# A graph network's attention pass: the second gather of each edge adds into the first by DMA, instead of a VectorE addition

## What is computed

```
x = x + _L2_gnn_ref(h, edge_attr_16, edge_attr_4, ..., edge_index)   # h: normalised x
# inside:
msg_s = (s_n @ Ws_src)[src] + (s_n @ Ws_dst)[dst]
msg_v = einsum(v_n, Wv_src)[src] + einsum(v_n, Wv_dst)[dst]
w1 = rbf @ W_rbf
m1_s, m1_v = _cg_tp(msg_s, msg_v, y0, y1, w1 ...)
a = leaky(m1_s @ W_alpha) * alpha_dot, summed by head      # scores
# values: two more linear maps, a gate and a second _cg_tp; softmax over the edges of a node; sum
```

## Time and profile before

| | |
|---|---|
| median of 3 runs | 6777.98 us |
| profiled execution, its own time | 6772.18 us |
| its span | 6767.9 us |
| PE busy | 6291.2 us (93%) |
| DVE busy | 4284.2 us (63%) |
| POOL busy | 4163.2 us (62%) |
| ACT busy | 2376.2 us (35%) |

### The profile page before, as it was taken

The page is one execution under the profiler, slowest core; times in us unless marked ns, Lnnn a source line. Parts: engine busy times, 40 slices in busy tenths (PEclk is TensorE's granted clock), DMA queues, the critical chain, the costliest instruction groups (busy, mean ns, idle before and its releaser), DMA issues. The chain is left out here.

```text
span 6767.9 us, 184764 instructions
## 1 busy us (share of the span) xinstructions
PE 6291.2 (93%) x57917; PEld 5076.0 (75%) x57917; DVE 4284.2 (63%) x11616; ACT 2376.2 (35%) x6454; POOL 4163.2 (62%) x4226
## 2 busy tenths in 40 slices
PE   6999999989999997999999999999288799999999
PEld 3788888777877775888888888888277448888887
DVE  5455555534444446999999999999488753333333
ACT  2122222212212124777777777777200121111111
POOL 1677777567777766777777777777000116666665
PEclk9999999989999997999999999999699559999999
DMA  1344444344444443333333333333167014444443
GB/s 60 111 120 124 124 123 122 108 114 129 127 123 129 126 106 87 97 96 95 95 97 96 95 95 97 96 95 96 52 185 194 4 47 115 115 115 115 115 116 97
DMA packets 735106, 719.47 MB, mean 106 GB/s; under 512 B 248938, under 2 KB 594266, under 8 KB 734338
## 3 DMA queue, kind: packets, MB, share of 16 engines
q1 hardware_dynamic: 546818, 396.43, 20.6%
q0 software_dynamic: 188160, 321.38, 19.0%
HBM read 557.59 MB, written 159.75 MB: 106 GB/s over the span
## 5 line engine op out<-in xcount | busy, mean ns | idle before, releaser
L892 POOL DMA_INDIRECT l_edge_g<-node_table,l_edge_idx x2352 | 2279.7, 969 | 1292.8 <-issue 944.1
L939 PEld LDWEIGHTS l_edge_win_ps<-l_edge_hot,l_edge_prod 128*128 128x128 f32 (+2 forms) x14112 | 1309.8, 149 | 218.2 <-issue 177.1
L939 PE MATMUL l_edge_win_ps<-l_edge_hot,l_edge_prod 128*128 128x40 f32 (+2 forms) x14112 | 1438.4, 255 | 36.0 <-DVE sums_T L752 24.7
L957 ACT ACTIVATE l_edge_h<-l_edge_h_ps 128x256 f32<-128x256 f32 (+1 forms) x784 | 342.9, 437 | 2753.0 <-PE l_edge_h_ps L913 2541.4
L1853 POOL DMA_INDIRECT att_g_dst<-node_table,att_ends x784 | 878.9, 1121 | 239.0 <-issue 239.0
L993 DVE TENSOR_TENSOR l_edge_prod<-l_edge_w_ps,l_edge_g 128x512 f32<-128x512 f32 x588 | 405.8, 690 | 961.3 <-PE l_edge_w_ps L920 812.2
L1851 POOL DMA_INDIRECT att_g<-node_table,att_ends x784 | 810.7, 1034 | 267.3 <-issue 238.1
L752 DVE TENSOR_TENSOR sums_T<-sums_T,l_edge_win_ps 128x160 f32 x588 | 189.4, 322 | 875.3 <-PE l_edge_win_ps L943 680.7
L1873 PE MATMUL att_turn<-ident,sums_T 128*128 128x128 f32 (+1 forms) x4704 | 690.0, 282 | 36.8 <-ACT sums_T L1958 29.9
L920 PEld LDWEIGHTS l_edge_w_ps<-l_edge_wo,l_edge_h 64*128 64x128 f32 (+1 forms) x4704 | 502.3, 190 | 286.9 <-issue 284.4
L1958 ACT ACTIVATE sums_T<-att_turn 128x512 f32<-128x512 f32 (+1 forms) x1176 | 661.8, 593 | 110.6 <-PE att_turn L1873 104.7
(11 more groups left out here) (272 smaller groups left out, 10086.0 us busy)
## 6 DMA issues: line engine op xcount, KB each, us to landing
l_edge_hot<-hot_tiles SPq DMA_DIRECT2D x392, 320.0 KB
hot_tiles<-l_edge_hot SPq DMA_DIRECT2D x196, 320.0 KB, 2.3
l_messages<-att_rows SPq DMA_DIRECT2D x196, 320.0 KB
sum_msg<-l_messages SPq DMA_DIRECT2D x196, 320.0 KB, 3.5
l_edge_g<-node_table,l_edge_idx POOLq DMA_INDIRECT x2352
att_ea<-in_edge_attr_T SPq DMA_DIRECT2D x196, 64.0 KB
att_g<-node_table,att_ends POOLq DMA_INDIRECT x784
att_g_dst<-node_table,att_ends POOLq DMA_INDIRECT x784
```

The costliest lines, as they stand in the source:

```text
L892: pool.indirect_dma_start(g[s][:, t, :], None, rows_of, bass.IndirectOffsetOnAxis(idx[s][:, t:t + 1], 0)).then_inc(fetched[s], 16)
L939: nc.tensor.matmul(at, q[:, t, lo:lo + width], to[:, t, kinds, :], start=t == 0, stop=t == TG - 1)
```

## The change

`g_dst` and DVE's `join` go. POOL first gathers all four source tiles of group i into `g[s]`. Then it waits until the source rows of group i-1 have landed, and issues four indirect DMAs that gather the destination rows of group i-1 and add them to `g` in flight (`compute_op=ALU.add`). The semaphore `joined` becomes four, one for each buffer, and counts landings of those DMAs (16 each); ACT, DVE and SP wait for it where they waited for `join` or for the fetch. POOL has one step more at the end.

```
-                g_dst = pair("g_dst", [P, TG, FEAT], n=FETCH)
-                joined = sem(ctx, "att_joined")
+                joined = [sem(ctx, f"att_joined{s}") for s in range(FETCH)]
...
-                                at_least(sp, fetched[s], 32 * TG * r)
+                                at_least(sp, joined[s], 16 * TG * r)
...
                                 for t in range(TG):
                                     pool.indirect_dma_start(g[s][:, t, :], None, table[2],
                                                             bass.IndirectOffsetOnAxis(ends[s][:, t:t + 1], 0)).then_inc(fetched[s], 16)
-                                    pool.indirect_dma_start(g_dst[s][:, t, :], None, table[3],
-                                                            bass.IndirectOffsetOnAxis(ends[s][:, TG + t:TG + t + 1], 0)
-                                                            ).then_inc(fetched[s], 16)
-
-                        steps(pool, NG, 0, step, warm=8, unroll=U)
+                            if live(i - 1, NG):
+                                s1, r1 = back(s, r, 1, U)
+                                gate(pool, (w_loaded, 16 * N_LOAD),
+                                     (fetched[s1], 16 * TG * (r1 + 1)))
+                                for t in range(TG):
+                                    pool.indirect_dma_start(g[s1][:, t, :], None, table[3],
+                                                            bass.IndirectOffsetOnAxis(ends[s1][:, TG + t:TG + t + 1], 0),
+                                                            compute_op=ALU.add).then_inc(joined[s1], 16)
+
+                        steps(pool, NG, 1, step, warm=8, unroll=U)
...
-                                 (joined, i + 1))
+                                 (joined[s], 16 * TG * (r + 1)))
...
-                        def join(i, s, r):
-                            at_least(dve, fetched[s], 32 * TG * (r + 1))
-                            tt(g[s][:, :, :], g[s][:, :, :], g_dst[s][:, :, :], ALU.add, joined)
-
...
-                            dve.wait_ge(joined, i + 1)
+                            at_least(dve, joined[s], 16 * TG * (r + 1))
...
-                        join(0, 0, 0)
-
...
-                            if live(i, NG) and live(i + 1, NG):
-                                join(i + 1, (s + 1) % U, r + (s + 1) // U)
...
-                        steps(dve, NG - 1, 4, step, warm=8, unroll=U)
+                        steps(dve, NG, 3, step, warm=8, unroll=U)
```

## The result

The changed kernel takes 7132.68 us (median of 4 runs, 7118.78 to 7139.69) against 6775.08 before (median of 4): a ratio of 1.0524, 95% interval 1.0505 to 1.0543, or 358 us more by the medians (355 by the ratio, which takes in all nine runs of the changed kernel). The forecast of 6782 was wrong, and so was the range, which ended at 7090. It is the first rival, POOL as the bound, that came true, above its likeliest value of 7003.

What follows compares the result with a forecast made beforehand. PE was taken to bound the kernel at 11.08 us a group. Profiled 6772.18 plus 4.2 for the start, other terms 0, gave 6776.4, or 6782 us against the median; range 6760 to 7090.

Steps and rivals of the forecast that it cites:

- the first rival: POOL's stream: adding DMAs lift its step above PE's 11.08 us a group; +225 us, 7003 us; chance 42%.
- PE paces before: Settled attention pass: PE sets the pace at 11.08 us a group, busy 10.85 and idle 0.23.
- The join is worth 0 on the path: DVE: removing 196 joins of 0.82 us only lengthens its wait for ACT's gate before `att_vec`; 0 us.
- The start, +4.2: Start of the pass: four more DMAs before group 0 (+5.0 us), less one join of 0.82; +4.2 us.
- The added wait and the later destination rows, 0: POOL's wait for source rows passes at once; destination rows land at 22.9 us, needed at 25.9; 0 us.
- The adding DMA, e of 0 to 0.19: POOL's extra time e per adding DMA over a plain one's 0.95 us, taken as 0 to 0.19 us.
- The break-even: POOL's step reaches PE's 11.08 us at e = 0.19, an adding DMA of 1.14 us.
- POOL's 10.31 without the extra: POOL's own time for eight plain DMAs a group, read between joins at the start of the pass: 10.31 us.
- The slower rival, 1.42 for three accesses instead of two: POOL's time goes by accesses described: adding DMA 1.42 us, e = 0.47, step 12.19; 7003 us; chance 42%.
- upper bound of e = 0.70: POOL's largest extra per adding DMA, from the longest gather of 1.647 us: +406 us, 7184 us.
- The transfer: DMA engines: ample room expected; a rival with adding DMAs ten times 0.32 us gave +575, 7357 us; chance 4%.
- The two-input rule: DVE instructions with two SBUF inputs slow POOL; removing the join could give POOL up to 0.69 us a group; not counted.

Runs made afterwards that it cites:

- the plain run: Changed kernel with the second gather of each tile overwriting instead of adding (no `compute_op`): 6769.64 us, ratio 0.9991.
- one-tile run: Kernel with one tile of four added by DMA and the other three by DVE's `join`: 6782.55 us, ratio 1.0011.
- 64-row runs: Changed kernel with second gathers of 64 rows instead of 128: adding 7077.25 us (ratio 1.0444), plain 6777.77 us.
- the runs without stands: Changed kernel with PE's `weigh` done twice a group, 7109.33 us; changed kernel with SP's score store one step later, 7105.64 us.

## Why the prediction was wrong, point by point

- **PE paces before: right.** Without the join the time is 9 us lower (3 to 16), and the trace puts 7 of them in the first five groups.
- **The join is worth 0 on the path: right in the settled pass**, and its time did turn into the wait for the gate. In the start it was worth some 7 us, where I had counted its 0.82 once.
- **The start, +4.2: right** for plain DMAs (4.1 by the rows of the plain run); in the changed kernel the four adding ones make it 6.7 (the first `att_vy` 2583.3 - 2564.1 = 19.2 us after the first gather instead of 12.5).
- **The added wait and the later destination rows, 0: right.** Ratio 0.9991.
- **The adding DMA, e of 0 to 0.19: wrong, and this is the step that failed.** It was taken "by the nearest row", the median gather, because rows, bytes and indices are the same. But e is 0.59 at the least and 0.57 between the page's means, 1.583 and 1.009. So POOL's step, which I put at 10.31 + 4e and below PE's 11.08, is 12.98 us, and POOL paces. The row nearest in kind said nothing of a different operation. The break-even was only a fifth of a gather's own time away, which asked for less trust in that choice.
- **POOL's 10.31 without the extra: too low.** The one-tile run has a step of 11.20 where it gives 10.9, because the plain DMAs are longer in the settled pass. So the room of 0.77 us a group was smaller than I took it.
- **The slower rival, 1.42 for three accesses instead of two: right in kind, low in size.** Its picture, time by number of accesses, falls with the 64-row runs: most of the extra is fixed. Its upper bound of e = 0.70 held the truth; I had cut the range at 0.58. With e = 0.63, the mean adding DMA over an undisturbed one, its formula gives 10.31 + 2.52 = 12.83 a step, x 191 = +334, 13 for the first five and 4: +351. That this comes so near 358 is partly luck: the sum has none of the stands below.
- **The range's other omission: the clock.** Some 20 to 27 us of the loss, by the runs without stands, is POOL standing behind late indices while PE is slow. I had named `first(i-4)` as POOL's gate; in the stands the later one is the load of `ends`.
- **The transfer: right that it doesn't matter.** By the estimate above an adding DMA holds an engine 0.69 us instead of 0.32, a factor of 2.2 and not ten.
- **The two-input rule** (the Trainium skill, SBUF — State Buffer, Who interferes with whom): I did not count POOL's relief from the join. It is real: by the means of the rows, the eight DMAs of a group take 0.54 us less without it (1.121 to 0.997 for a destination gather, 1.034 to 1.024 for a source one). In that run it became POOL's standing. In the kernel before, gathers that start beside the join take 1.56 us on the mean (3000 to 4600 us), those beside `att_vy` out of `g` 1.30, those beside the four `att_p` of `second` 1.01. Why these last, which also read two SBUF operands, stretch so little stays unexplained.

## What to carry to other kernels

An operation moved to DMA was paid for here by the engine that issues it; before counting what the freed engine saves, sum the issuing engine's step and see how far it is from the pace (here 0.8 us for four DMAs, against 2.4 needed). Where a price is unknown and the margin is small, ask first at which price the answer turns over, and doubt the nearest row if it is of another operation. And when an engine that paces is overtaken by another, look at whatever stands in order behind it on a third queue: a small index load behind a store cost about 0.3% here.

## What the runs showed of the hardware that I had not expected

In these runs an indirect DMA costs POOL much the same whatever it moves: 0.893 us at least for 64 rows and 0.942 for 128; adding, 1.403 and 1.532, and 1.531 with half the bytes. An adding one of 128 rows makes 144 packets where a plain one makes 48, and with 64 rows it is 80 against 32: 16 and one for each row, against 16 and one for every four rows. PE's granted clock fell to 0.50 in stretches although PE was busy 19.03 of the 20 us before (3380 to 3400) and 18.25 in the 20 in which it fell; with two adding tiles, PE busy 469.49 of 500 us, it kept 1.00.
